# TensorE's order in a group of keys: row scores of the next step ahead of the values product of the preceding group

## Chip, cores, metric

One core of one Trainium2 chip. The metric is device time of one execution, in microseconds; the kernel before ran three times.

## What is computed

A small language model tower on 8 sequences of 1024 tokens, width 512, all in float32:

```python
h = embed(x)                       # gathered frequencies, phases, amplitudes; sin, cos; projection
n = layernorm(h)
Q, K, V = split(n @ q_w.T + q_b), ...          # 16 heads of 32
S = einsum('hid,hjd->hij', K, Q) * SCALE       # K's rows are the rows of the softmax
S = where(i < j, -inf, S) - (i - j)            # causal, with a decay by distance
h = h + softmax(S) @ V @ o_w.T + o_b
h = h + shared_expert(layernorm(h)) + top_6_of_32_experts(layernorm(h))
```

## The kernel before

Three parts run one after the other: `embed`, `attend`, `experts`. The change lies in `attend`.

Attention runs in 32 steps: 8 batches by G = 4 sets g of 4 heads (HG = 4). A step has N_GROUPS = 12 groups m of keys, each a pair (half of the rows, tile j of 128 keys): groups 0 to 3 belong to the first half, groups 4 to 11 to the second. The widths are 512, 384, 256, 128, then 512 five times, then 384, 256, 128. Groups on the diagonal (0 to 3 and 8 to 11) are masked by one more matmul per head.

For each group TensorE (function `step` at L1325) issues:
- `scores` (L1199): keys by rows for each head, K = 32 rows of the array (L1212), the row shift (L1216) and, if masked, the mask (L1222), in four banks of a ring of six.
- `attend_group` (L1225): the values product of the *preceding* group (L1235), out of the exponentials that ScalarE made.
- `row_scores` (L1180): scores of the *next* step, rows by keys (L1188), in four banks of the same ring. VectorE takes their maxima (`row_maxima`, L893, L898), which give the shift of the next step's softmax.
- three gaps A, B, C for dense work in one bank, `ps_dense`, by the tables PROJECT_AT, OUT_AT, QUARTER_AT and so on at L383 to L391: projections of the head set two steps on (L1172 for v, L1176 for q and k), sums of the exponentials (L1244), maxima turned to rows (L1195), and the residual work of the batch before, one quarter of its rows per step: output projection (L1253, g = 0 only), `turn` (L1261), `route` (L1268), `up` (L1276, at m = 6 and 8), `place` (L1292) and `down` (L1284, at m = 11). The first batch has no such residual work.

The bank of the ring decides the waits. Scores of group m take positions 8m to 8m+3, row scores 8m+4 to 8m+7, all modulo 6:

```python
def score_bank(m, h): return ps_ring[(2 * HG * m + h) % RING]
def row_bank(k, h): return ps_ring[(2 * HG * k + HG + h) % RING]
...
if h == 2 and after_exp is not None:
    pe.wait_ge(exp_done, after_exp)
```

So row scores of heads 2 and 3 (L1186) wait for the exponentials of heads 0 and 1 of the same group, and scores of heads 2 and 3 of the next group (L1210) wait for the first two row maxima of this one. Each dense piece waits until the preceding one has been taken out of `ps_dense` (`dense_free`).

ScalarE (`step` at L835) does per group exponentials of heads 0 and 1, gap A, heads 2 and 3 (L776), then at m = 0 and 4 it takes the finished heads (`take_heads`, L783), then gaps B and C. VectorE (`step` at L1104) takes gaps A and B, the four row maxima (L898), a division (L919, L922), then the residual work (`tail_events`: at m = 6 `soft_sum`, L970 to L982; at m = 7 and 10 `gate`, L1056 to L1065; at m = 8 `choose`), then gap C (at m = 7 and 9 the copy of the values, L890; at m = 10 `find_places`, L1030). GpSimd adds the exponentials of a group to those of its first group (L714), four per group, and scatters rows (L718). SyncE moves the residual rows.

Of the kernel before, what the change touches and what calls it, by code (L numbers as in the profile page):

```python
# [36 lines left out]
G = H * HD // P  # L37
HG = H // G
# [15 lines left out]
def wait_from_1(eng, sem, value):  # L54

    if isinstance(value, int) and value <= 0:
        return
    eng.wait_ge(sem, value)
# [309 lines left out]
ITEMS = HG * N_GROUPS  # L368
# [13 lines left out]
A, B, C = range(3)  # L382
# [101 lines left out]
def attend(nc, io, dram):  # L484
    with ExitStack() as ctx:
# [96 lines left out]
        def row_shape(k):  # L582

            i, c = ROW_TILES[k]
            return i, c, c * HALF, min((i + 1) * P, (c + 1) * HALF) - c * HALF
# [4 lines left out]
        def row_bank(k, h):  # L590
            return ps_ring[(2 * HG * k + HG + h) % RING]
# [568 lines left out]
        def _(pe):  # L1160
# [3 lines left out]
            def project(g, kind, half, n):  # L1164

                wait_from_1(pe, dense_free, n)
                w = {"q": q_w, "k": k_w, "v": v_w}[kind]
                if kind == "v":
                    for t in range(NT // 2):
                        tile = half * NT // 2 + t  # L1170
                        for c in range(DC):
                            mm = nc.tensor.matmul(ps_dense[:, t * P:(t + 1) * P], normed_t[:, c, tile * P:(tile + 1) * P],  # L1172
                                                  w[:, c, g * P:(g + 1) * P], start=(c == 0), stop=(c == DC - 1))
                else:
                    for c in range(DC):
                        mm = nc.tensor.matmul(ps_dense[:], w[:, c, g * P:(g + 1) * P], normed_t[:, c, half_cols(half)],  # L1176
                                              start=(c == 0), stop=(c == DC - 1))
                mm.then_inc(dense_full, 1)

            def row_scores(s, g, k, after_exp=None):  # L1180

                i, c, j0, width = row_shape(k)
                wait_from_1(pe, rows_done, ITEMS * s + HG * k)
                for h in range(HG):
                    if h == 2 and after_exp is not None:
                        pe.wait_ge(exp_done, after_exp)  # L1186
                    dims = slice(h * HD, (h + 1) * HD)
                    nc.tensor.matmul(row_bank(k, h)[:, 0:width], k_t[g][dims, i * P:(i + 1) * P],  # L1188
                                     q_t[g][dims, j0:j0 + width], start=True, stop=True).then_inc(rows_full, 1)

            def turn_maxima(s, half, n):
                wait_from_1(pe, dense_free, n)
                pe.wait_ge(max_done, 2 * s + half + 1)
                for i in range(NT // 2):
                    mm = nc.tensor.matmul(ps_dense[:, i * P:(i + 1) * P], max_cols[:, half * NT // 2 + i, :], ident_b[:],  # L1195
                                          start=True, stop=True)
                mm.then_inc(dense_full, 1)

            def scores(st, m):  # L1199

                half, j, i0, width = shape(m)
                masked = j * P == i0
                wait_from_1(pe, exp_done, ITEMS * st.s + HG * m)
                if st.first and m == 0:
                    pe.wait_ge(dense_free, N_PROLOGUE)
                if m == HALF_GROUPS:
                    pe.wait_ge(dense_free, st.number("maxima", 1) + 1)
                for h in range(HG):
                    if h == 2 and (st.rows or m < 2):
                        pe.wait_ge(rows_done, ITEMS * (st.s + 1) + (HG * m - 2 if st.rows or m == 0 else 0))  # L1210
                    dims = slice(h * HD, (h + 1) * HD)
                    nc.tensor.matmul(score_bank(m, h)[:, 0:width], q_t[st.g][dims, j * P:(j + 1) * P],  # L1212
                                     k_t[st.g][dims, i0:i0 + width], start=True, stop=False)
                for h in range(HG):
                    dims = slice(h * HD, h * HD + SHIFT)
                    mm = nc.tensor.matmul(score_bank(m, h)[:, 0:width], key_shift[dims, j * P:(j + 1) * P],  # L1216
                                          row_shift[st.g % 2][dims, i0:i0 + width], start=False, stop=not masked)
                    if not masked:
                        mm.then_inc(scores_full, 1)
                if masked:  # L1220
                    for h in range(HG):
                        nc.tensor.matmul(score_bank(m, h)[:, 0:P], mask_b[:], ident_b[:], start=False,  # L1222
                                         stop=True).then_inc(scores_full, 1)
# [15 lines left out]
            def sum_probs(s, half, n):  # L1239

                wait_from_1(pe, dense_free, n)
                pe.wait_ge(added, ADDS * s + (ADDS if half else EARLY_ADDS))
                for h in range(HG):
                    mm = nc.tensor.matmul(ps_dense[h * HD:(h + 1) * HD, :], ones[:], first_probs[half][h][:],  # L1244
                                          start=True, stop=True)
                mm.then_inc(dense_full, 1)

            def out_project(t, i, n):
                wait_from_1(pe, dense_free, n)

                pe.wait_ge(heads_done, 2 * G * t + 2 * G - (1 if i < NT // 2 else 0))
                for g in range(G):
                    mm = nc.tensor.matmul(ps_dense[:], attn_t[:, g, i * P:(i + 1) * P], o_w[:, g, :],  # L1253
                                          start=(g == 0), stop=(g == G - 1))
                mm.then_inc(dense_full, 1)
# [41 lines left out]
            def of_quarter(x, p, kind, arg, n):  # L1297
                if kind == "turn":
                    turn(x, p, arg, n)
                elif kind == "route":  # L1300
                    route(n)
                elif kind == "up":
                    up(arg, n)
                elif kind == "down":
                    down(x, arg, n)
                elif kind == "place":
                    count_earlier(x, n)

            def dense(st, slot, gap):
                for kind, arg, k in st.uses[slot][gap]:  # L1310
                    n = st.base + k
                    if kind in ("q", "k", "v"):
                        if st.g == 2 and (kind, arg) == PROJECTIONS[0]:
                            pe.wait_ge(normed_in, 16 * (st.b + 2))
                        project((st.g + 2) % G, kind, arg, n)
                    elif kind == "sums":
                        sum_probs(st.s - 1 if arg else st.s, arg, n)
                    elif kind == "maxima":
                        turn_maxima(st.s if arg else st.s + 1, arg, n)
                    elif kind == "out":  # L1320
                        out_project(st.t, arg, n)
                    else:
                        of_quarter(QUARTERS * st.t + st.g, st.g % 2, kind, arg, n)

            def step(st):  # L1325
                for m in range(N_GROUPS):
                    scores(st, m)
                    dense(st, m, A)
                    if m > 0:
                        attend_group(st.s, st.g, m - 1)  # L1330
                    elif not st.first:
                        attend_group(st.s - 1, (st.g - 1) % G, N_GROUPS - 1)
                    dense(st, m, B)
                    if st.rows:
                        row_scores(st.s + 1, (st.g + 1) % G, m, ITEMS * st.s + HG * m + 2)
                    dense(st, m, C)

            pe.wait_ge(normed_in, 16)
            for n, (kind, half) in enumerate(PROJECTIONS * 2):
                project(n // N_PROJ, kind, half, n)  # L1340
                if n >= N_PROJ:
                    for k in range(2):
                        row_scores(0, 0, 2 * (n - N_PROJ) + k)
            turn_maxima(0, 0, N_PROLOGUE - 1)
            for_batches(pe, step)
            attend_group(FINAL - 1, G - 1, N_GROUPS - 1)
            sum_probs(FINAL - 1, 1, EPILOGUE_SUMS)
# [288 lines left out]
```

## Time and profile before

| | us |
|---|---|
| median of 3 runs | 4180.8 (4173.16 to 4185.16) |
| profiled execution | 4192.13 |
| its span | 4190.3 |
| TensorE busy | 3459.1 |
| VectorE busy | 2486.1 |
| GpSimd busy | 1812.4 |
| ScalarE busy | 1043.1 |

A row of the timeline gives the start, the duration, the engine, line, operation, output and inputs, shape and how many instructions it merges; in brackets the idle time of the engine ahead of it and what released it. Matmuls of four heads run side by side, so that a merged row is shorter than the sum of its parts. An fp32 matmul is two instructions (x8 for four heads). The attention part lies between about 615 and 3680 us.

### The profile page before, as it was taken

The page shows a single profiled execution, that of the slowest core. Times are in us where ns is not written, and L with a number is a line of the kernel's source. Part 1 is how long each engine was busy: PE and PEld are TensorE (multiplying, and loading weights), DVE is VectorE, ACT ScalarE, POOL GpSimd, SP SyncE. Part 2 cuts the span into 40 slices and gives each one's busy share as a digit, 9 for nine tenths or more (in the row PEclk, how much of TensorE's full clock was granted, in tenths as well). Part 3 has the DMA queues.
Part 4 walks back from the last instruction along what each step waited for, and adds up shares of the span by engine and source line. Part 5 has one row for each costly group of instructions (what it writes and reads, how often), then busy time and mean ns, then how long its engine had stood idle before and what let it go on. Part 6 is the DMA issues. An engine that isn't in the chain of part 4 may idle for free. (4 is left out here: it accounts for less than half of the span.)

```text
span 4190.3 us, 65616 instructions
## 1 busy us (share of the span) xinstructions
PE 3459.1 (83%) x20360; PEld 1725.1 (41%) x20360; DVE 2486.1 (59%) x6671; ACT 1043.1 (25%) x2427; POOL 1812.4 (43%) x1892
## 2 busy tenths in 40 slices
PE   5676479999888988888898889888988897754998
PEld 1222133444444444343444444444444443233776
DVE  3555434555665676567656665666576567643565
ACT  1111103332332223232223322332232222200111
POOL 3322204544554455355444544554455455522223
PEclk6555589999999999998999999999999997876999
DMA  4444300001111110100011010001000100111997
GB/s 158 142 151 156 146 31 1 26 26 40 63 48 63 41 35 12 49 18 27 22 41 41 11 34 29 31 12 37 26 32 11 46 16 11 44 38 57 264 258 166
DMA packets 123228, 257.99 MB, mean 62 GB/s; under 512 B 38988, under 2 KB 39628, under 8 KB 120192
## 3 DMA queue, kind: packets, MB, share of 16 engines
q1 hardware_dynamic: 78832, 204.56, 14.8%
q0 software_dynamic: 44048, 49.26, 4.7%
q8 instruction: 161, 2.64, 0.3%
q14 instruction: 187, 1.53, 0.1%
HBM read 146.71 MB, written 204.26 MB: 84 GB/s over the span
## 5 line engine op out<-in xcount | busy, mean ns | idle before, releaser
L714 POOL TENSOR_TENSOR a_first_probs<-a_first_probs,a_probs 128x512 f32<-128x512 f32 (+3 forms) x1280 | 1176.0, 953 | 1526.9 <-ACT a_probs L776 943.5
L898 DVE CUSTOM_DVE_ANT_0 a_unused<-a_ps_ring,a_decay 128x512 bf16<-128x512 f32 (+3 forms) x1536 | 773.6, 554 | 593.7 <-PE a_ps_ring L1188 585.0
L776 ACT ACTIVATE a_probs<-a_ps_ring 128x512 f32<-128x512 f32 (+3 forms) x1280 | 505.0, 473 | 752.2 <-PE a_ps_ring L1222 555.5
L718 POOL DMA_INDIRECT d_slots<-a_rows,a_place_i x397 | 394.8, 994 | 250.4 <-DVE a_place_i L1050 142.2
L1212 PE MATMUL a_ps_ring<-a_k_t,a_q_t 32*128 32x512 f32 (+3 forms) x3072 | 416.4, 542 | 71.5 <-DVE a_row_max L898 47.3
L1188 PE MATMUL a_ps_ring<-a_q_t,a_k_t 32*128 32x512 f32 (+3 forms) x3072 | 390.4, 542 | 17.4 <-DVE a_row_max L898 12.4
L1284 PE MATMUL a_ps_dense<-a_sd,a_inner_t 128*128 128x512 f32 x256 | 185.3, 863 | 184.4 <-DVE a_gate_up L1030 181.1
L1176 PE MATMUL a_ps_dense<-a_normed_t,a_q_w 128*128 128x512 f32 x512 | 242.4, 617 | 44.9 <-DMA a_normed_t<-d_normed_t 42.2
L1235 PE MATMUL a_ps_heads<-a_probs,a_values 128*32 128x512 f32 (+3 forms) x2560 | 269.9, 495 | 0.0
L1212 PEld LDWEIGHTS a_ps_ring<-a_k_t,a_q_t 32*128 32x128 f32 x3072 | 146.3, 186 | 275.5 <-issue 147.9
L1253 PE MATMUL a_ps_dense<-a_o_w,a_attn_t 128*128 128x512 f32 x512 | 241.3, 615 | 16.8 <-DVE a_values L890 9.0
L776 ACT ACTIVATE a_first_probs<-a_ps_ring 128x512 f32<-128x512 f32 x256 | 135.7, 605 | 471.0 <-PE a_ps_ring L1222 444.9
L1176 PE MATMUL a_ps_dense<-a_normed_t,a_k_w 128*128 128x512 f32 x512 | 238.5, 609 | 15.9 <-DVE a_residual L929 10.0
L1172 PEld LDWEIGHTS a_ps_dense<-a_v_w,a_normed_t 128*128 128x128 f32 x2048 | 235.1, 193 | 36.5 <-issue 33.8
L1172 PE MATMUL a_ps_dense<-a_v_w,a_normed_t 128*128 128x128 f32 x2048 | 247.3, 279 | 1.6 <-DVE a_values L890 0.9
L919 DVE RECIPROCAL a_sum_inv<-a_sum_inv 128x128 f32<-128x128 f32 x256 | 242.5, 947 | 1.9 <-ACT a_sum_inv L789 1.9
L1188 PEld LDWEIGHTS a_ps_ring<-a_q_t,a_k_t 32*128 32x128 f32 x3072 | 143.4, 187 | 225.1 <-issue 189.2
L1276 PE MATMUL a_ps_dense<-a_rows_t,a_sg 128*128 128x256 f32 x512 | 161.1, 469 | 79.0 <-DVE a_values L890 73.3
L1550 POOL DMA_INDIRECT out<-x_y,x_index x64 | 90.1, 1409 | 236.4 <-DMA out<-x_y,x_index 184.6
L912 DVE CAST a_row_shift<-a_ps_dense 128x512 bf16<-128x512 f32 x64 | 44.2, 691 | 240.6 <-PE a_ps_dense L1195 240.6
L1284 PEld LDWEIGHTS a_ps_dense<-a_sd,a_inner_t 128*128 128x128 f32 x256 | 59.7, 258 | 266.2 <-DVE a_inner_t L1065 150.5
L1276 PEld LDWEIGHTS a_ps_dense<-a_rows_t,a_sg 128*128 128x128 f32 x512 | 112.1, 230 | 125.3 <-DVE a_values L890 76.9
(169 smaller groups left out, 4653.7 us busy)
## 6 DMA issues: line engine op xcount, KB each, us to landing
d_hidden<-e_hidden SPq DMA_DIRECT2D x8, 2048.0 KB, 7.4
d_normed_t<-e_normed_t SPq DMA_DIRECT2D x8, 2048.0 KB, 11.8
a_normed_t<-d_normed_t SPq DMA_DIRECT2D x8, 2048.0 KB, 7.7
a_residual<-d_hidden SPq DMA_DIRECT2D x64, 256.0 KB, 2.7
d_hidden<-a_residual SPq DMA_DIRECT2D x64, 256.0 KB, 2.1
a_hidden<-d_hidden SPq DMA_DIRECT2D x64, 256.0 KB, 2.7
out<-a_hidden SPq DMA_DIRECT2D x64, 256.0 KB, 2.0
x_w_gate<-w_gate SPq DMA_DIRECT2D x32, 512.0 KB, 6.5
```

The source lines that it names most:

```text
L714: nc.gpsimd.tensor_tensor(total_of, total_of, probs_of(m, h)[:, 0:width], ALU.add).then_inc(added, 1)
L718: nc.gpsimd.indirect_dma_start(slot_rows, bass.IndirectOffsetOnAxis(ap=place_i[p][:, j, choice:choice + 1], axis=0), rows[p][:, j, :], Non ...
L776: nc.scalar.activation(probs_of(m, h)[:, 0:width], score_bank(m, h)[:, 0:width], ACT.Exp).then_inc(exp_done, 1)
L898: nc.vector.tensor_tensor_reduce(unused[:, h, 0:width], row_bank(k, h)[:, 0:width], decay[:, at:at + width], 1.0, NEG, ALU.add, ALU.max, r ...
L919: nc.vector.reciprocal(sum_inv[half][:, cols], sum_inv[half][:, cols]).then_inc(sums_inverted, 1)
L1172: mm = nc.tensor.matmul(ps_dense[:, t * P:(t + 1) * P], normed_t[:, c, tile * P:(tile + 1) * P], w[:, c, g * P:(g + 1) * P], start=(c == 0 ...
L1176: mm = nc.tensor.matmul(ps_dense[:], w[:, c, g * P:(g + 1) * P], normed_t[:, c, half_cols(half)], start=(c == 0), stop=(c == DC - 1))
L1188: nc.tensor.matmul(row_bank(k, h)[:, 0:width], k_t[g][dims, i * P:(i + 1) * P], q_t[g][dims, j0:j0 + width], start=True, stop=True).then_i ...
L1212: nc.tensor.matmul(score_bank(m, h)[:, 0:width], q_t[st.g][dims, j * P:(j + 1) * P], k_t[st.g][dims, i0:i0 + width], start=True, stop=False)
L1235: mm = nc.tensor.matmul(ps_heads[dims, at], values[g][:, j, dims], probs_of(m, h)[:, 0:width], start=(j == 0), stop=(j == last_j))
L1276: mm = nc.tensor.matmul(ps_dense[:, k * 2 * P:(k + 1) * 2 * P], w[:, c, m * P:(m + 1) * P], rows_t[:, c, :], start=(c == 0), stop=(c == DC ...
L1284: mm = nc.tensor.matmul(ps_dense[:], inner_t[:, m, j * P:(j + 1) * P], sd[:, m, :], start=(m == 0), stop=(m == MC - 1))
```

## The change

In each group `row_scores` and gap B move ahead of `attend_group`: before, scores, A, values product, B, row scores, C; now, scores, A, row scores, B, values product, C.

```diff
                     scores(st, m)
                     dense(st, m, A)
+                    if st.rows:
+                        row_scores(st.s + 1, (st.g + 1) % G, m, ITEMS * st.s + HG * m + 2)
+                    dense(st, m, B)
                     if m > 0:
                         attend_group(st.s, st.g, m - 1)
                     elif not st.first:
                         attend_group(st.s - 1, (st.g - 1) % G, N_GROUPS - 1)
-                    dense(st, m, B)
-                    if st.rows:
-                        row_scores(st.s + 1, (st.g + 1) % G, m, ITEMS * st.s + HG * m + 2)
                     dense(st, m, C)
```

TensorE, group 8 of a step with g = 1 in the loop over batches, and the `up` piece behind it (L1276), before:

```order
L1216 MATMUL a_ps_ring<-a_row_shift,a_key_shift 128x512 x4
L1222 MATMUL a_ps_ring<-a_ident_b,a_mask_b 128x128 x4
L1235 MATMUL a_ps_heads<-a_probs,a_values 32x512 x4
L58 REGISTER_ALU
L1188 MATMUL a_ps_ring<-a_q_t,a_k_t 128x128 x4
L58 REGISTER_ALU
L1276 MATMUL a_ps_dense<-a_rows_t,a_sg 128x256 x4
```

Now:

```order
L1216 MATMUL a_ps_ring<-a_row_shift,a_key_shift 128x512 x4
L1222 MATMUL a_ps_ring<-a_ident_b,a_mask_b 128x128 x4
L58 REGISTER_ALU
L1188 MATMUL a_ps_ring<-a_q_t,a_k_t 128x128 x4
L1235 MATMUL a_ps_heads<-a_probs,a_values 32x512 x4
L58 REGISTER_ALU
L1276 MATMUL a_ps_dense<-a_rows_t,a_sg 128x256 x4
```

The row scores stand directly behind the mask, and the values product between them and `up`.

TensorE, group 4 of the same step, with the two pieces `turn` (L1261) in gaps A and B and the scores of group 5 behind it, before:

```order
L1261 MATMUL a_ps_dense<-a_ident,a_rows 128x128 x4
L1235 MATMUL a_ps_heads<-a_probs,a_values 32x128 x4
L58 REGISTER_ALU
L1259 REGISTER_ALU
L1261 MATMUL a_ps_dense<-a_ident,a_rows 128x128 x4
L58 REGISTER_ALU
L1188 MATMUL a_ps_ring<-a_q_t,a_k_t 128x512 x4
L1212 MATMUL a_ps_ring<-a_k_t,a_q_t 128x512 x2
```

Now:

```order
L1261 MATMUL a_ps_dense<-a_ident,a_rows 128x128 x4
L58 REGISTER_ALU
L1188 MATMUL a_ps_ring<-a_q_t,a_k_t 128x512 x4
L58 REGISTER_ALU
L1259 REGISTER_ALU
L1261 MATMUL a_ps_dense<-a_ident,a_rows 128x128 x4
L1235 MATMUL a_ps_heads<-a_probs,a_values 32x128 x4
L1212 MATMUL a_ps_ring<-a_k_t,a_q_t 128x512 x2
```

The row scores no longer stand directly ahead of the next group's scores; `turn` and the values product lie between them. The orders of the other four engines are the same.

## Rows read from the trace of the kernel before

**Rows 1.** The page, part 1: busy us, share of the span, instructions.

```profile
PE 3459.1 (83%) x20360; PEld 1725.1 (41%) x20360; DVE 2486.1 (59%) x6671; ACT 1043.1 (25%) x2427; POOL 1812.4 (43%) x1892
```

**Rows 2.** Waits of PE, 700 to 3600 us: total, times, longest.

```profile
PE a_ps_dense L1284 <- DVE a_gate_up L1030: 164.1, 27, 6.3
PE a_ps_dense L1276 <- DVE a_values L890: 73.3, 19, 4.0
PE a_ps_ring L1212 <- DVE a_row_max L898: 42.8, 57, 3.8
```

**Rows 3.** Timeline of PE, group 6 of a step with g = 3.

```profile
2033.67 1.14 PE L1212 MATMUL a_ps_ring<-a_k_t,a_q_t 32*128 32x512 f32 x8
2034.63 0.40 PE L1216 MATMUL a_ps_ring<-a_row_shift,a_key_shift 5*128 5x512 bf16 x4
2034.96 1.07 PE L1235 MATMUL a_ps_heads<-a_probs,a_values 128*32 128x512 f32 x8
2035.95 1.36 PE L1188 MATMUL a_ps_ring<-a_q_t,a_k_t 32*128 32x512 f32 x8
2037.24 1.99 PE L1276 MATMUL a_ps_dense<-a_rows_t,a_sg 128*128 128x256 f32 x8
```

**Rows 4.** Timeline of ACT, exponentials of group 6 of that step.

```profile
2035.05 2.06 ACT L776 ACTIVATE a_probs<-a_ps_ring 128x512 f32<-128x512 f32 x4 [3.83 <-PE a_ps_ring L1216]
```

**Rows 5.** Timelines of PE and of ACT, group 9 of that step.

```profile
2061.78 0.40 PE L1222 MATMUL a_ps_ring<-a_ident_b,a_mask_b 128*128 128x128 bf16 x4
...
2063.10 0.71 PE L1188 MATMUL a_ps_ring<-a_q_t,a_k_t 32*128 32x256 f32 x8
2063.75 3.84 PE L1172 MATMUL a_ps_dense<-a_v_w,a_normed_t 128*128 128x128 f32 x32
...
2062.05 1.64 ACT L776 ACTIVATE a_probs<-a_ps_ring 128x384 f32<-128x384 f32 x4 [0.31 <-PE a_ps_ring L1222]
```

**Rows 6.** Timeline of PE, turn at m = 4 and scores of group 5, same step.

```profile
2022.54 0.66 PE L1261 MATMUL a_ps_dense<-a_ident,a_rows 128*128 128x128 f32 x4 [0.28 <-DVE a_rows L954]
2027.24 0.70 PE L1212 MATMUL a_ps_ring<-a_k_t,a_q_t 32*128 32x512 f32 x2 [0.69 <-DVE a_row_max L898]
```

**Rows 7.** Timeline of PE, `up` at m = 8, same step.

```profile
2055.42 3.68 PE L1276 MATMUL a_ps_dense<-a_rows_t,a_sg 128*128 128x256 f32 x8 [4.00 <-DVE a_values L890]
```

**Rows 8.** Timeline of DVE, from the maxima of group 6 to the values copy.

```profile
2037.26 0.69 DVE L898 CUSTOM_DVE_ANT_0 a_unused<-a_ps_ring,a_decay 128x512 bf16<-128x512 f32 x1 [1.53 <-PE a_ps_ring L1188]
...
2043.05 1.31 DVE L978 TENSOR_TENSOR a_soft<-a_soft_ln,a_soft 128x64 f32<-128x64 f32 x1
...
2053.53 1.24 DVE L1065 TENSOR_SCALAR a_inner_t<-a_gate_e 128x256 f32<-128x256 f32 x1
2054.69 0.68 DVE L890 COPY a_values<-a_ps_dense 128x512 f32<-128x512 f32 x1
```

**Rows 9.** Timeline of DVE, the same lines in the next step, g = 0.

```profile
2155.51 0.22 DVE L978 TENSOR_TENSOR a_soft<-a_soft_ln,a_soft 128x64 f32<-128x64 f32 x1
...
2166.86 0.29 DVE L1065 TENSOR_SCALAR a_inner_t<-a_gate_e 128x256 f32<-128x256 f32 x1
```

**Rows 10.** Timeline of POOL, additions of groups 7 and 8, g = 3.

```profile
2043.03 4.94 POOL L714 TENSOR_TENSOR a_first_probs<-a_first_probs,a_probs 128x512 f32<-128x512 f32 x4
...
2050.55 5.34 POOL L714 TENSOR_TENSOR a_first_probs<-a_first_probs,a_probs 128x512 f32<-128x512 f32 x4 [1.43 <-ACT a_probs L776]
```

**Rows 11.** Timeline of DVE, division at m = 10 (g = 3) and at m = 6 (g = 0).

```profile
2073.39 1.50 DVE L922 TENSOR_TENSOR a_attn_t<-a_attn_t,a_sum_inv 128x128 f32<-128x128 f32 x1
...
2154.09 0.29 DVE L922 TENSOR_TENSOR a_attn_t<-a_attn_t,a_sum_inv 128x128 f32<-128x128 f32 x1
```

**Rows 12.** Timeline of PE, k projection at m = 4, g = 2.

```profile
2326.81 3.70 PE L1176 MATMUL a_ps_dense<-a_normed_t,a_k_w 128*128 128x512 f32 x8 [0.16 <-ACT a_rows_t L800]
```

**Rows 13.** Timeline of PE, output projection at m = 8, g = 0.

```profile
2167.82 3.70 PE L1253 MATMUL a_ps_dense<-a_o_w,a_attn_t 128*128 128x512 f32 x8 [1.30 <-DVE a_values L890]
```

**Rows 14.** Timeline of PE, scores of group 11, first batch.

```profile
684.23 0.38 PE L1212 MATMUL a_ps_ring<-a_k_t,a_q_t 32*128 32x128 f32 x2 [1.06 <-DVE a_row_max L898]
```

## The prediction

> **What bounds the kernel now.** I read the page first: over the whole span TensorE is busy 83%, VectorE 59% [rows 1]. The profiled execution took 4192.1 us (span 4190.3), against a median of 4180.8 for the runs; the sum below is made against 4192.1 and its difference is then taken off the median. Next, the table of waits on PE for 700 to 3600 us [rows 2]: the shared-expert product `down` waits 164.1 us for VectorE, `up` waits 73.3 us in 19 places, key scores wait 42.8 us for row maxima. So inside a group of keys TensorE runs without a gap, and a few times per step it stands for VectorE. I then walked the timeline of one step (the fourth batch, g=3, 1993.68 to 2087.90) and of its neighbours; g=1 and g=3 have the same pattern ("odd steps"). Below, S(m) is the start of the scores of group m.
>
> **What one exchange costs.** Group 6 [rows 3]: scores at 2033.67, shift matmuls at 2034.63, values product at 2034.96, row scores at 2035.95, the next product at 2037.24: 3.57 us. ScalarE starts the four exponentials at 2035.05 and needs 2.06 us, 0.515 each [rows 4]. Row scores of heads 2 and 3 go into the banks of scores 0 and 1, so they wait for two exponentials: 2035.05 + 1.03 + 0.05 = 2036.13. Before, the 0.99 us of the values product covered this. Now row scores of heads 0 and 1 start at 2034.96, heads 2 and 3 at 2036.13; a 512 wide pair takes 1.06 more, then the values product 0.99: 2038.18. Group 6 pays **0.96**, practically the whole values product. Group 9 [rows 5]: mask at 2061.78, exponentials of 384 columns from 2062.05, two of four in 1.64 done at 2062.92, 256 wide row scores to 2063.56, product to 2064.55 where the old order had 2063.75: **0.80**. The same working on the other widths gives 0.36 (m=0), 0.57 (m=2), 0.37 (m=3), 0.98 (m=7), 1.00 (m=8), 0.59 (m=10). Where a dense piece stands in gap A (sums at m=1 and 5, turn at 4, `down` at 11, the output projections of g=0) it covers the exponentials and I cost the exchange at nothing; without that piece it would be 0.4 to 1.0 as above. No instruction is added; DMA, ScalarE, VectorE and GpSimd keep their orders.
>
> **What comes back, odd steps.**
> Groups 0 to 3: nothing; +0.36+0.57+0.37 = +1.3.
> Groups 4 and 5: before, scores(5) started directly behind row scores(4) and its heads 2 and 3 stood until VectorE had two row maxima, at 2027.24 [rows 6]. Now row scores(4) end near 2024.4 (heads 0 and 1 reach VectorE about 2024.2), turn(1) and the 128 wide values product follow, scores(5) starts at 2025.4 and finds its maxima done, ending 2026.7 instead of 2028.5. Sums 0.88, row scores to 2028.95, maxima 0.33, product 0.98, router 1.90 put S(6) at about 2032.1, not 2033.67: -1.57; with 1.3 us already lost, turn(0) no longer waits 0.28 for VectorE. Together -1.85.
> Groups 6 to 8: paid 0.96+0.98+1.00 = 2.94. But `up` of m=8 stands 4.00 us for the copy of the values [rows 7], and behind that stand the granted clock is at its lower level: eight matmuls take 3.68 us where the same eight of m=6 take 1.99 at the upper one [rows 3, 7], and the clock comes back within them: 1.7 lost. Will the copy be early enough? VectorE's chain starts with the row maxima of group 6, at S(6)+3.59 (2037.26), and runs without idle time into the copy, ending near S(6)+21.7 [rows 8]. Row scores of heads 0 and 1 now end at S+2.3, so the chain starts at S(6)+2.45, 1.14 earlier. Its slow operations are slow beside GpSimd's additions: L978 takes 1.31 there and 0.22 in g=0, L1065 1.24 and 0.29 [rows 8, 9]. The additions of group 8 start at S(6)+16.9 now [rows 10] and follow the exponentials, which TensorE's later groups 6 and 7 move to S(6)+18.9; the gate's last three operations then lie ahead of them, 1.15 us in place of 3.4 us. The copy ends about S(6)+18.3, while TensorE only gets there at 17.7+2.94 = 20.6. Stand and low clock go: 2.94-4.00-1.70 = -2.8.
> Groups 9 to 11: VectorE sits idle in group 9 for TensorE, and gets each row maximum 1.0 earlier after S(9) while group 10 starts 0.80 later: the maxima of group 10 start at S(9)+9.7 as before, and `down` in group 11 still stands for this chain, at the lower clock. In it L922 took 1.50 beside GpSimd's last additions and 0.29 elsewhere [rows 11]; these additions start some 0.7 later, so between 0 and -1.2; I take -0.35, since the operation behind L922 can meet them instead.
> Odd step: 1.3-1.85-2.8-0.35 = **-3.7**.
>
> **Other steps.** g=2: group 0 already waits for its exponentials, +0.94 up to group 3. At m=4 the k projection waits for ScalarE's turned rows, before 0.16 [rows 12]; ScalarE takes the heads ahead of them, and the heads' last values product now comes after turn(1), so this wait grows: +0.8 together with m=5. Then -2.8-0.35: **-1.4**. g=0: the same +0.8, then the stand of 1.30 at the output projection of m=8 [rows 13] shrinks by 1.0 and the row maxima of m=10 come 0.8 earlier: **-1.0**. A batch: 2 x -3.7 - 1.4 - 1.0 = -9.8, six full batches -59. Last batch: its `up` stands little, some groups gain, some pay: 0. First batch, without residual work: exposures 0.57+0.37+0.36+1.10+0.35+0.80+0.36 = 3.9, against waits of PE for row maxima that go (1.06 [rows 14], 0.69 twice, 0.44): +1 per step, +4. **Sum: -59 + 4 = -55 us**: 4137 for the profiled execution, 4126 for the median.
>
> **A rule weighed.** L978 lasts 1.31 us while additions run on GpSimd and 0.22 without [rows 8, 9]. The Trainium skill ("SBUF — State Buffer", section on the two separate sides) says that VectorE and GpSimd lock a shared port pair for a whole instruction, the other one blocking fully; the two rows agree. It speaks against this change where more of the chain falls into additions: a rival below.
>
> **The rivals.**
> (1) Forecast, 4126: chance 0.54.
> (2) More operations blocked: the chain starts earlier against the additions of group 6, so that L970, L972, L975 and L1056 each take 1.0 more. Copy at S(6)+22.3, `up` stands 1.7 without losing the clock: 18 x 1.7 = +31, 4157. For: L978 to L982 do it today. Against: L1065 and L1061 leave the additions. 0.10. By the page on SBUF of the Trainium skill each meeting costs up to a whole addition, here 4.94/4 = 1.24 us [rows 10]; the stand would be 2.6 and the time 4173.
> (3) The clock stays down: short stands in every group lower TensorE's activity and the granted clock of groups 6 to 9 falls as it does now: 18 x 1.7 = +31, 4157. Against: its clock is full through the present groups with stands of 0.7. 0.14.
> (4) Slower: the exposures are paid and the values copy is no earlier. Its place is the 18 stands of `up` at m=8: if GpSimd's additions hold VectorE's chain so that the copy ends at S(6)+21.7 again, S(9) stays where it is and only the small terms are left: odd -0.55, g=2 +1.7, g=0 +0.8, batch +1.4; six batches and the first: +13, 4194. It decides once the copy gains less than 0.7 us. 0.10.
> (5) Larger gain: L922's block is gone everywhere (-0.85 more in 24 steps): -20, 4105. 0.12.
> That the change does nothing is excluded by the order on PE.
>
> **Numbers.** The range goes from (5) with some more, 4090, to past (2) and (3), 4172; (4) is left out above. A measurement here tells 0.3% (12.5 us) from no change. Slower by more takes most of (4): 0.09; within 0.07; faster 0.84.
>
> **What would show it.** Right: the wait of L1276 for L890 (19 times) nearly gone and the granted clock of that stretch at full; the wait of L1212 for L898 below 15 us; a new wait of L1188 for ScalarE's L776, some 0.2 us each, and row scores taking over 2 us from first to last; L898 starting 2.45 us behind the scores; `down` standing as before, about 5.5 us. Wrong: L1276 still waiting over 2 us (4), or a stretch at half clock without a long stand ahead of it (3).

## The result, and the profile after

The changed kernel takes 4268.9 us (median of 4 runs, 4264.3 to 4274.9) against 4178.7 for the kernel before (with a fourth run): ratio 1.0216, 95% interval 1.0194 to 1.0238. It is **2.2% slower**, where 4126 us was forecast. Its profiled execution has a span of 4263.4 us. Part 1 of its page, against [rows 1]:

```profile
PE 3571.5 (84%) x20360; PEld 1763.6 (41%) x20360; DVE 2566.6 (60%) x6671; ACT 1048.8 (25%) x2427; POOL 1822.0 (43%) x1892
```

The instruction counts are unchanged, but VectorE is busy 80.5 us longer. An operation that is held back counts as busy, so this is the first hint. The table of waits of PE, 700 to 3600 us, against [rows 2] (total, times, longest):

```profile
PE a_ps_dense L1284 <- DVE a_gate_up L1030: 157.6, 26, 6.3
PE a_ps_dense L1276 <- DVE a_values L890: 54.7, 19, 3.0
PE a_ps_ring L1188 <- ACT a_probs L776: 30.9, 87, 0.7
PE a_ps_dense L1176 <- ACT a_rows_t L800: 15.7, 13, 1.3
PE a_ps_ring L1188 <- ACT a_first_probs L776: 13.8, 25, 0.6
PE a_ps_ring L1212 <- DVE a_row_max L898: 6.3, 19, 1.7
```

Row maxima are waited for 6.3 us instead of 42.8, as forecast. Row scores now wait for ScalarE, which was forecast too, at some 0.2 us each; it is 0.4. What fails is the second row: `up` still waits for the values copy in the same 19 places, 2.9 us each, and after the exposed exponentials have been paid.

**Where the time went, by group.** The starts of the scores (L1212) give the length of each group. Means over the six full batches of the profiled executions, us, change minus before (the twelfth column runs to the next step's scores):

```
step   m=0   1     2     3     4     5     6     7     8     9     10    11     sum   forecast
g=0   -0.73 +0.14  0.00 -0.84 +0.83 +0.35  0.00  0.00 -1.00  0.00 +0.64 -1.13  -1.7   -1.0
g=1   +0.36 +0.14 +0.64 +0.42 -0.11 -1.35 +0.99 +0.99 +1.38 +0.85 +0.64 -1.41  +3.5   -3.7
g=2    0.00 -0.12 +0.64 +0.43 +0.82 +0.35 +0.99 +1.00 +1.85 +0.85 +0.29 -0.97  +6.1   -1.4
g=3   +0.36 +0.14 +0.64 +0.42 -0.10 -1.35 +1.00 +1.00 +1.33 +0.85 +0.64 -1.62  +3.3   -3.7
```

A batch is 11.2 us longer, six are 67 us; the first batch adds 1.4, and the first scores start 3.4 later (614.7, 618.1). That is 72 of the 73.1 us between the two spans. The 3.4 us need not be due to the change: in experiments 1 to 10, none of which touches the part ahead of attention, the first scores start anywhere between 607.1 and 619.3. Column m=8 carries the surprise: in g=1 to 3 it should have been about -4.7, and is +1.3 to +1.9.

The timeline of PE in the same step as [rows 3, 7] (fourth batch, g=3; S(6) = 2064.89):

```profile
2064.89 1.14 PE L1212 MATMUL a_ps_ring<-a_k_t,a_q_t 32*128 32x512 f32 x8
...
2067.40 1.13 PE L1188 MATMUL a_ps_ring<-a_q_t,a_k_t 32*128 32x512 f32 x4 [0.31 <-ACT a_probs L776]
2068.45 1.07 PE L1235 MATMUL a_ps_heads<-a_probs,a_values 128*32 128x512 f32 x8
...
2082.82 0.70 PE L1212 MATMUL a_ps_ring<-a_k_t,a_q_t 32*128 32x512 f32 x2 [0.26 <-DVE a_row_max L898]
...
2090.01 3.61 PE L1276 MATMUL a_ps_dense<-a_rows_t,a_sg 128*128 128x256 f32 x8 [3.02 <-DVE a_values L890]
```

Group 6 pays just the 1.0 us that was worked out. But `up` of m=8 stands 3.02 us, and its eight matmuls take 3.61 us, much as in [rows 7]. The stand is 0.98 us shorter than before, and still group 8 takes 13.83 us instead of 12.53. Two terms make up for it: its own exposed exponentials, 1.0 us, and 1.4 us in its scores, whose heads 2 and 3 now meet late row maxima of group 7 (the mask matmuls start 2.66 us behind S(8), where it was 1.29). VectorE and GpSimd show why; first VectorE, against [rows 8]:

```profile
2070.92 3.62 DVE L922 TENSOR_TENSOR a_attn_t<-a_attn_t,a_sum_inv 128x128 f32<-128x128 f32 x1
...
2075.39 5.19 DVE L975 TENSOR_TENSOR a_soft<-a_soft,a_soft_w 128x64 f32<-128x64 f32 x1
2080.62 0.29 DVE L978 TENSOR_TENSOR a_soft<-a_soft_ln,a_soft 128x64 f32<-128x64 f32 x1
...
2088.12 1.23 DVE L1065 TENSOR_SCALAR a_inner_t<-a_gate_e 128x256 f32<-128x256 f32 x1
2089.28 0.68 DVE L890 COPY a_values<-a_ps_dense 128x512 f32<-128x512 f32 x1
```

Then GpSimd's additions of groups 5, 6 and 7:

```profile
2063.33 4.93 POOL L714 TENSOR_TENSOR a_first_probs<-a_first_probs,a_probs 128x512 f32<-128x512 f32 x4 [10.96 <-PE a_ps_heads L1235]
...
2069.42 4.95 POOL L714 TENSOR_TENSOR a_first_probs<-a_first_probs,a_probs 128x512 f32<-128x512 f32 x4
2074.54 0.99 POOL L718 DMA_INDIRECT d_slots<-a_rows,a_place_i  x1 [0.17 <-issue]
2075.54 4.95 POOL L714 TENSOR_TENSOR a_first_probs<-a_first_probs,a_probs 128x512 f32<-128x512 f32 x4
```

In the kernel before, the same two engines (S(6) = 2033.67):

```profile
2030.71 4.94 POOL L714 TENSOR_TENSOR a_first_probs<-a_first_probs,a_probs 128x512 f32<-128x512 f32 x4 [10.59 <-PE a_ps_heads L1235]
...
2036.81 4.97 POOL L714 TENSOR_TENSOR a_first_probs<-a_first_probs,a_probs 128x512 f32<-128x512 f32 x4
...
2040.70 1.24 DVE L922 TENSOR_TENSOR a_attn_t<-a_attn_t,a_sum_inv 128x128 f32<-128x128 f32 x1
...
2042.80 0.22 DVE L975 TENSOR_TENSOR a_soft<-a_soft,a_soft_w 128x64 f32<-128x64 f32 x1
```

Read the ends. L922 ends some 0.16 us behind the end of group 6's four additions in both kernels (2074.54 and 2074.37; 2041.94 and 2041.78). L975 of the change ends at 2080.58, behind the last addition of group 7 (2080.49): an operation of 0.22 us waited out a whole run of four. The copy so ends at S(6)+25.1, where 18.3 was forecast and 21.7 was before.

And read the starts. The run of group 5 begins 2.96 us ahead of the scores of group 6 before, and 1.56 us after. It is released by the values product of group 4, by these lines of `add_probs` (group 5 has j = 1; other lines are left out):

```python
if j == 1:
    pool.wait_ge(attended, N_GROUPS * st.s + m)
...
for h in range(HG):
    pool.wait_ge(exp_done, ITEMS * st.s + HG * m + h + 1)
```

In group 5 that is the product which the change moved behind the row scores. The runs of groups 6 and 7 follow with only one scatter (L718, 0.99 us) between them. It is the rule and not this step: in each of the 18 steps with g=1 to 3 of the six full batches the run of group 5 starts 2.96 us ahead of S(6) before and 1.56 now, and L975 lasts 0.22 to 0.23 us before and 5.19 to 5.21 now. Over all its 32 executions L975 went from 12.6 to 102.0 us.

### The profile page after: what moved, and what is told of

Same layout as the page of the kernel before. It is cut to its first block and busy times, and to the rows that moved or that the text cites. A ratio compares the mean times of both kernels' runs of the same rounds, so it can differ in the third digit from the quotient of the medians.

```text
span 4263.4 us, 65610 instructions
## 1 busy us (share of the span) xinstructions
PE 3571.5 (84%) x20360; PEld 1763.6 (41%) x20360; DVE 2566.6 (60%) x6671; ACT 1048.8 (25%) x2427; POOL 1822.0 (43%) x1892
## 5 line engine op out<-in xcount | busy, mean ns | idle before, releaser
L1188 PE MATMUL a_ps_ring<-a_q_t,a_k_t 32*128 32x512 f32 (+3 forms) x3072 | 528.9, 542 | 60.3 <-ACT a_probs L776 32.7
L718 POOL DMA_INDIRECT d_slots<-a_rows,a_place_i x397 | 396.7, 999 | 250.9 <-DVE a_place_i L1050 142.9
L1212 PE MATMUL a_ps_ring<-a_k_t,a_q_t 32*128 32x512 f32 (+3 forms) x3072 | 395.3, 542 | 27.6 <-DVE a_row_max L898 10.0
L1188 PEld LDWEIGHTS a_ps_ring<-a_q_t,a_k_t 32*128 32x128 f32 x3072 | 201.3, 189 | 332.3 <-issue 152.4
L1176 PE MATMUL a_ps_dense<-a_normed_t,a_k_w 128*128 128x512 f32 x512 | 240.2, 612 | 21.6 <-ACT a_rows_t L800 15.7
L1212 PEld LDWEIGHTS a_ps_ring<-a_k_t,a_q_t 32*128 32x128 f32 x3072 | 133.0, 185 | 224.5 <-issue 158.5
L1276 PE MATMUL a_ps_dense<-a_rows_t,a_sg 128*128 128x256 f32 x512 | 167.6, 484 | 60.3 <-DVE a_values L890 54.7
L922 DVE TENSOR_TENSOR a_attn_t<-a_attn_t,a_sum_inv 128x128 f32<-128x128 f32 x256 | 165.1, 645 | 13.6
L1276 PEld LDWEIGHTS a_ps_dense<-a_rows_t,a_sg 128*128 128x128 f32 x512 | 117.2, 241 | 132.7 <-DVE a_values L890 74.2
```

What stands on the lines that cost most here:

```text
L718: nc.gpsimd.indirect_dma_start(slot_rows, bass.IndirectOffsetOnAxis(ap=place_i[p][:, j, choice:choice + 1], axis=0), rows[p][:, j, :], Non ...
L1276: mm = nc.tensor.matmul(ps_dense[:, k * 2 * P:(k + 1) * 2 * P], w[:, c, m * P:(m + 1) * P], rows_t[:, c, :], start=(c == 0), stop=(c == DC ...
```

## The experiments

Two theories stood. Port (P in the first texts, R, as "release", in the last ones): VectorE's waits beside GpSimd's additions take back what groups 6 to 8 should give. Exposure (E): the exposed exponentials cost more than was summed.

**1, 2: additions of 128 columns.** Both orders, with the additions of groups 6 and 7 cut from 512 to 128 columns, so that these two kernels leave out most of those additions and their softmax sums are not the right ones:

```
                 at = slice(HALF - width, HALF)
+                if m in (6, 7):
+                    width, at = 128, slice(HALF - 128, HALF)
```

> The order of the change, and GpSimd's additions of groups 6 and 7 act on 128 of the 512 columns (the rest of these sums is left out). Theory P (port): the values copy is late in the changed kernel because L922 (3.6 us) and L975 (5.2 us) wait out whole runs of additions. With short runs the copy ends near S(6)+19, the stand of `up` at m=8 (3.02 us) and its clock loss go, and the stretch S(6) to S(9) falls from 30.4 to 24.3 us in 18 steps: about 4160 us. Theory E (the exposed exponentials alone cost the time): the stretch keeps its stand, 4255 to 4270 us.

> The order of before with the same short additions of groups 6 and 7 (part of these sums left out). Theory P: four VectorE operations lose 1.0 us each, the copy ends near S(6)+17.6, the stand of 4.0 us shrinks to about nothing and the clock stays up: S(6) to S(9) from 27.1 to about 21.4 us, some 4080 us. The distance between this run and e1 is then the bare price of the exposed exponentials, 50 to 80 us. Theory E: 4170 to 4180.

New order 4136.7 us (ratio 0.9883, 0.9852 to 0.9913), old order 4067.9 (0.9727, 0.9662 to 0.9792). The wait of `up` for the values copy is gone from both. Theory P had asked for some 4160 and 4080. Short additions are worth 132 us to the new order and 111 to the old. With them out of the way the new order costs 69 us net: the exposed exponentials where there is no stand at m=8 to take away, less what the new order gains elsewhere (1.35 us in group 5 of each odd step, for one).

**3: the new order in all groups but 6 to 8.** In this and the next ones the order has both forms, and a condition chooses:

```
+                    rows_first = m < 6 or m > 8
                     scores(st, m)
                     dense(st, m, A)
+                    if st.rows and rows_first:
+                        row_scores(st.s + 1, (st.g + 1) % G, m, ITEMS * st.s + HG * m + 2)
+                    if rows_first:
+                        dense(st, m, B)
...
+                    if not rows_first:
+                        dense(st, m, B)
+                    if st.rows and not rows_first:
```

> The new order in groups 0 to 5 and 9 to 11, the old one in groups 6 to 8. Theory P: the loss sits in groups 6 to 8, and what is left is the rest of the change: per batch about -2 (g=0), -1 for each odd step, +2 (g=2): 4165 to 4185 us. Theory E: each exposed group costs its 0.4 to 0.8 us wherever it is, +2.7 us in 18 steps: about 4225 us.

4286.6 us (1.0250, 1.0184 to 1.0316): slower than the full change, and both theories missed. Groups 6 and 7 are as before, and group 8 is 3.1 to 4.6 us longer than before. Its L975 takes 111.9 us in all. So the block is not made by the order in groups 6 to 8, but brought to them from ahead: here too the run of group 5 starts 1.56 us ahead of S(6).

**4, 5: a gap between additions.** Each addition waits for the end of the one before it, in both orders:

```
-                    wait_from_1(pool, added, ADDS * st.s + HG * (later(m) - 1) + h + 1)
+                    wait_from_1(pool, added, ADDS * st.s + HG * later(m) + h)
```

> The order of the change, and every addition on GpSimd waits for the one before it, so that they are not queued back to back. Theory P with a lock that GpSimd keeps only while its next addition is already waiting: L922 and L975 get in after one addition (at most 1.3 us), the copy ends near S(6)+20, the stand goes: about 4165 us. If VectorE is held for the whole run all the same, or under theory E: 4265 to 4285 us.

> The order of before, and every addition on GpSimd waits for the one before it (the edit of e4). Theory P: in the order of before no VectorE operation waits for more than one addition, so the gaps give little there: 4160 to 4185 us, and the new order with gaps (4133) is then really the faster one. Rival: the gaps help either order by the same 130 us: about 4050 us.

The new order falls to 4133.0 us (0.9883, 0.9821 to 0.9944); the old one rises to 4234.8 (1.0126, 1.0106 to 1.0146). Both forecasts missed: 4165 and 4160 to 4185 were expected. In the six full batches no operation of the chain lasts over 2 us any more, and the longest of all is 2.1; L975 is 0.84 us in the median of the new order. But several are now held by an addition that they meet. In the new order the copy is in time all the same, at S(6)+18.6, and group 8 takes 7.76 us, 4.7 to 5.0 less than before. In the old one L972, L975, L978, L980 and L982 last 1.2 to 2.0 us each, the copy ends at S(6)+23.8 or later, and group 8 grows by 2.1 to 3.0 us.

**6: a mixture by the small terms.** `rows_first = m < 8 if st.t is None else st.g == 0 or (st.g % 2 == 1 and m == 4)`: the new order in group 4 of the steps g=1 and 3, in all groups of g=0, and in groups 0 to 7 of the first batch.

> The new order only in all groups of g=0 with residual work, in group 4 of g=1 and g=3, and in groups 0 to 7 of the first batch; elsewhere the order of before. Theory P: values product 4 in group 5 and with it GpSimd's additions keep their place before the scores of group 6, nothing is blocked for a whole run; g=0 gains 2.7, odd steps 1.5 each: -5.7 per batch and a few us in the first: 4140 to 4150 us. If group 4 in the new order is enough to shift the additions into VectorE's chain: 4200 or more.

4183.2 us over 10 runs (1.0005, 0.9993 to 1.0018): nothing, where 4140 to 4150 was expected. Group 5 of the odd steps gives its 1.33 us, but group 8 of the steps g=1 to 3 takes 0.6 to 0.8 back, g=0 gains 1.4 us instead of 2.7, and g=2 loses 1.9. Without the gain at m=8 the rest is worth little.

**7, 8: all groups but 5, and only 6 to 8.** `rows_first = m != 5` and `rows_first = m >= 6 and m <= 8`.

> The new order in all groups but 5, where the values product of group 4 (which releases GpSimd's additions of group 5) keeps its place ahead of the row scores. Theory P with this release as the cause: the additions of groups 5 to 7 run 1.4 us earlier against the scores of group 6, L922 or L975 lose at most one addition each: 4150 to 4220 us. If the release is not what matters: 4265 us as the change.

> The new order only in groups 6 to 8 of every step. Theory P with the release of GpSimd in group 5 as the cause: additions stay in place, VectorE's chain starts 1.1 us earlier and meets only the end of the additions of group 6; the stand of `up` at m=8 shrinks by what the exposures (2.9 us) add: 4120 to 4190 us. If starting VectorE's chain earlier is by itself what gets it blocked: 4240 us or more.

4138.2 us (0.9897, 0.9871 to 0.9922; 4150 to 4220 expected) and 4134.6 (0.9888, 0.9858 to 0.9918), two runs each, as in experiments 2 to 4. **Taking one group of twelve out of the change turns +2.2% into -1.0%.** In both, groups 6, 7 and 8 of the odd steps stand at +1.00, +0.99, -4.73: -2.74 us, where -2.8 was forecast. The chain of experiment 8, g=3 of the fourth batch, S(6) = 2001.93, VectorE, GpSimd, TensorE:

```profile
2011.06 0.23 DVE L975 TENSOR_TENSOR a_soft<-a_soft,a_soft_w 128x64 f32<-128x64 f32 x1
...
2011.84 0.20 DVE L982 TENSOR_SCALAR a_soft<-a_soft 128x64 f32<-128x64 f32 x1
...
2019.21 0.68 DVE L890 COPY a_values<-a_ps_dense 128x512 f32<-128x512 f32 x1
...
1998.98 4.93 POOL L714 TENSOR_TENSOR a_first_probs<-a_first_probs,a_probs 128x512 f32<-128x512 f32 x4 [10.58 <-PE a_ps_heads L1235]
...
2012.29 5.00 POOL L714 TENSOR_TENSOR a_first_probs<-a_first_probs,a_probs 128x512 f32<-128x512 f32 x4 [1.09 <-ACT a_probs L776]
...
2022.60 1.99 PE L1276 MATMUL a_ps_dense<-a_rows_t,a_sg 128*128 128x256 f32 x8
```

Group 5's run starts 2.95 us ahead of S(6). GpSimd then has to wait 1.09 us for the exponentials of group 7, and in that hole L975 to L982 pass at 0.2 us each. The copy ends at S(6)+17.96, TensorE finds it done, and the eight matmuls take 1.99 us.

**9: only group 5 in the new order** (`rows_first = m == 5`).

> The order before, with the new order in the one group m=5 of every step: there the values product of group 4, which releases GpSimd's additions of group 5, comes after the row scores. Theory R (the moved release alone does it): those additions start some 1.4 us nearer to the scores of group 6 (1.55 us ahead of them, where it was 2.96), L975 or L922 waits out a whole run of four additions in the steps g=1 to 3, group 8 grows from 12.5 us by 3 to 5.5 us in each, as in the kernel with the new order in all groups but 6 to 8: 54 to 99 us in six batches, 4235 to 4280 us. Rival A (it takes the new order in the groups 0 to 4 or 9 to 11 as well): nothing but the exposed exponentials of one group, 4175 to 4195 us.

4278.2 us (1.0217, 1.0191 to 1.0243): one group is enough for a loss as large as that of the whole change. The same view of it, S(6) = 2077.53, with TensorE:

```profile
2075.98 4.95 POOL L714 TENSOR_TENSOR a_first_probs<-a_first_probs,a_probs 128x512 f32<-128x512 f32 x4 [12.17 <-PE a_ps_heads L1235]
...
2084.56 2.65 DVE L922 TENSOR_TENSOR a_attn_t<-a_attn_t,a_sum_inv 128x128 f32<-128x128 f32 x1
2088.07 5.19 DVE L975 TENSOR_TENSOR a_soft<-a_soft,a_soft_w 128x64 f32<-128x64 f32 x1
...
2095.50 0.70 PE L1212 MATMUL a_ps_ring<-a_k_t,a_q_t 32*128 32x512 f32 x2 [2.27 <-DVE a_row_max L898]
```

The additions start 1.55 us ahead of S(6). Group 5 itself costs only 0.17 to 0.36 us, since the sums in gap A cover its exponentials; group 8 grows by 3.7 to 4.5.

The block is the same, but it is paid for in another place than in the whole change, so that the equal totals are in part chance. TensorE reaches the scores of group 8 earlier against VectorE's chain and stands 2.27 us for the row maxima of group 7, where it stood 0.26 in the change. The granted clock falls behind that stand and is at its lower level (0.50 of full) from 2096.2 to 2106.4, 10.2 us; in the kernel before it was so for 3.4 us of the same step (2055.5 to 2058.9), behind the stand of `up`. The waits of PE (700 to 3600 us) for row maxima and for the values copy come to 115.9 us here and 116.1 before, so the loss is not in their sum; it goes with the longer stretch at the lower clock. In experiments 3 and 11 the clock is low for 10.2 and 13.7 us of this step.

**11, 12: GpSimd alone made late.** TensorE's order untouched (the old one, and that of experiment 8); GpSimd runs 2, 4 and 6 tiny chained additions on a scratch tile ahead of those of group 5 in the steps g=1, 2 and 3:

```
+                if m == 5:
+                    for k in range(2 * st.g):
+                        nc.gpsimd.tensor_tensor(idle, idle, idle, ALU.add).then_inc(idled, 1)
+                        pool.wait_ge(idled, 12 * st.b + st.g * (st.g - 1) + k + 1)
```

> The order before, TensorE untouched; GpSimd alone runs 2, 4 and 6 tiny chained additions on a scratch tile ahead of the additions of group 5 in the steps g=1, 2 and 3, each an estimated 0.25 to 0.3 us, so that these start about 0.5, 1.1 and 1.6 us later. Theory R: at the delay that is nearest to 1.4 us, VectorE's L922 and L975 wait out whole runs of additions (3 to 5 us) though no TensorE instruction has moved, and group 8 grows by 2 us or more; at the smallest delay it need not. Rival A (the block comes of TensorE's order): L922 stays under 1.6 us and L975 at 0.22 us, group 8 within 1.5 us of 12.5 in all three.

> The new order in the groups 6 to 8 alone, the version of 4134.6 us, with the same delays of GpSimd in the steps g=1, 2 and 3. Theory R: at a delay near 1.4 us L975 takes some 5 us again, the copy of the values comes late and group 8 grows from 7.76 us to 13 or more, what the full change shows. Rival A: group 8 stays within 1.5 us of 7.76 in all three steps.

One execution each: 4245.6 and 4214.1 us, so that the evidence here is the traces and not these times. The additions of group 5 start 0.56, 1.13 and 1.70 us later in g=1, 2 and 3. In the fourth batch, group 8 and L975 (L981 in these two):

```
                  old order: group 8   L975      new 6 to 8: group 8   L975
no delay          12.53                0.22      7.76                  0.23
g=1, 0.56 late    15.32                5.20      7.76                  0.22
g=2, 1.13 late    15.66                5.19      12.57                 0.23
g=3, 1.70 late    18.34                5.19      14.20                 5.18
```

Over the six full batches L975 is as in the table in every step, to 0.02 us. Group 8 varies in the old order: 15.3 to 15.7, 15.7 to 16.1, 15.9 to 18.3; in the other one it is 7.76, 11.1 to 12.6, 14.2 to 15.5.

From experiment 12, VectorE and GpSimd, g=2 and then g=3:

```profile
1963.40 0.23 DVE L981 TENSOR_TENSOR a_soft<-a_soft,a_soft_w 128x64 f32<-128x64 f32 x1
1963.66 1.28 DVE L984 TENSOR_TENSOR a_soft<-a_soft_ln,a_soft 128x64 f32<-128x64 f32 x1
...
2059.05 5.18 DVE L981 TENSOR_TENSOR a_soft<-a_soft,a_soft_w 128x64 f32<-128x64 f32 x1
...
2059.20 4.94 POOL L720 TENSOR_TENSOR a_first_probs<-a_first_probs,a_probs 128x512 f32<-128x512 f32 x4
```

So the cause is shown without moving a single instruction of TensorE: additions that start late make the block. The old order has no room, since 0.56 us is enough; the order with the hole in groups 6 to 8 stands 0.56 and fails at 1.13, there with the division (L928 here, L922 above) held for 3.35 us and single additions behind it (1.28 us on L984, 1.2 on the two that follow), at 1.70 with a whole run. I had thought that 0.56 us might be harmless in the old order too.

**10: the parts that pay.** `rows_first = st.t is not None and ((m >= 6 and m <= 8) or (st.g % 2 == 1 and m == 4))`: groups 6 to 8 behind the first batch, where experiment 8 had lost 11 us, and group 4 of the odd steps.

> The new order only in the groups 6 to 8 of the steps behind the first batch, and in group 4 of the steps g=1 and 3. The kernel with 6 to 8 alone took 4134.6; its first batch was 11 us longer than before's, which goes; group 4's new order takes 1.4 us out of group 5 in two steps of each of six batches, 17 us. Theory R (nothing here moves GpSimd's additions of group 5 against the scores of group 6): 4105 to 4115 us. Rival A (the shift by group 4 meets the gate's chain elsewhere, as group 8 of g=1 grew by 1.1 us where group 4 alone was changed): 4120 to 4135 us.

**4109.9 us**, 5 runs (4104.9 to 4110.9), ratio 0.9820, 0.9801 to 0.9839: 72 us below the kernel before, and below all versions that compute the whole. A batch is 13.1 us shorter, 2.7 of it in group 5 of the two odd steps, where the stand of [rows 6] has gone.

## Why the prediction was wrong

**The step that failed** is the one on groups 6 to 8: "The copy ends about S(6)+18.3". What TensorE pays and gets back was sized right (paid 0.96 and 0.98 in groups 6 and 7, measured 1.00 and 0.99; net -2.8, measured -2.74 in experiments 7 and 8), but it comes only while GpSimd's runs lie where they lay. The text said "DMA, ScalarE, VectorE and GpSimd keep their orders", which is so, and took the order for the times: the values product was costed as work that is moved on TensorE, and not as a release. In group 5 it releases a run of GpSimd that then goes on back to back through three groups. That cost +1.38 and +1.33 in place of about -4.7 at m=8, 6.1 us a step, and 6.6 in g=2: over 18 steps some 113 of the 143 us between 4126 and 4269. Of the rest, 13 us are the other groups of these batches (a whole batch: +11.2, where -9.8 was forecast). 15 more are no fault of the sum: it was made against a profiled execution 11 us above its median, while that of the change lies 4 below its own.

That the copy ends at S(6)+17.96 in experiment 8, where 18.3 was worked out, is in part luck. Two terms came out: the chain starts 1.20 us earlier (forecast 1.14), and the gate's last three operations save 2.2 (forecast 2.25). The others were not in the sum and nearly cancel: L978, L980 and L982 are held for no addition and save 3.0, while L922 takes 1.0 longer, L1056 0.7, and the row maxima wait 0.9 for row scores of the late group 7 and heads 2 and 3.

The kernel before could have warned. In its last batch, which the rows did not cover, VectorE is held for a run, or the rest of one, already: L1061 for 4.42 us (3531.93), L972 for 5.57 (3599.03) and L975 as follows:

```profile
3605.09 5.63 DVE L975 TENSOR_TENSOR a_soft<-a_soft,a_soft_w 128x64 f32<-128x64 f32 x1
3605.68 4.96 POOL L714 TENSOR_TENSOR a_first_probs<-a_first_probs,a_probs 128x512 f32<-128x512 f32 x4
```

**Rival (2)** named the right mechanism, with a wrong size: one addition for each of four operations, at most 1.24 us. Measured were 3.6 us for one and 5.2 us for another. **Rival (4)** gave the right sign and its condition, a copy that gains less than 0.7 us, was met: it ended 3.4 us later than before. It was priced at +13 with a chance of 0.10 because I let the copy be at worst as late as before; that it could gain less than nothing was not considered. The range ended at 4172 because (4) was left out of it, and its 4194 would have been 75 us short too.

**Rival (3)**, the clock: refuted. The granted clock of 900 to 3600 us is 0.95 in the change and 0.93 before, and groups 6 and 7 run at full clock.

**What held.** The chain starts 2.39 us behind S(6), forecast 2.45. Groups 0 to 3 of the odd steps: +1.56, forecast +1.3. Groups 4 and 5: -1.46, forecast -1.85. Row scores wait for ScalarE, 44.7 us in 112 places. Row maxima: 6.3 us, forecast under 15. Groups 4 and 5 of g=2: +1.17, forecast +0.8. Groups 9 to 11 of the odd steps: 0.0 instead of -0.35. The first batch: +1.4 for +4. g=0: -1.7 for -1.0, by luck: m=8 gave the -1.00 that was worked out, but groups 0 and 3 gave 1.6 us that were in no sum, groups 4 and 5 cost 1.2 instead of 0.8, and groups 9 to 11 gave 0.5 instead of 0.8.

## What to carry to other kernels

When an instruction is moved, list the semaphores that it increments and who waits on them, on engines too that are far from the critical path; the work that it releases moves with it. Where two engines hold each other off, price a shift of one against the other from both sides, and try the change group by group: here one of twelve groups made +2.2% out of a kernel that was ready to give -1.0%. And look in all steps of the old trace for the rare times that an operation takes long: three holds in the last batch showed at what price VectorE can meet GpSimd.

## What the runs showed of the hardware

A VectorE operation that meets a run of GpSimd additions can be held for the whole rest of the run: 5.19 us for an operation of 0.22, behind four additions of 1.24. The Trainium skill ("SBUF — State Buffer", the section on the two sides) has the pair of ports locked for the length of an instruction; these rows go beyond one instruction, and the measurement decides. Elsewhere the same operations pass after one addition each (1.31, 1.19, 1.16 us for L978, L980, L982 before).

What decides between the two is open. In the 18 steps each L975 of the change that was held for 5.2 us was recorded 0.14 to 0.16 us ahead of the run's first addition, and 0.23 to 0.24 us ahead it passed in the kernel before. The distance alone does not decide: in the six steps g=2 of experiment 12 it passed at 0.14 to 0.16, and the L975 of 5.63 us above was recorded 0.59 us ahead. In one step of the change L975 passed and the next operation was held instead:

```profile
3509.64 0.23 DVE L975 TENSOR_TENSOR a_soft<-a_soft,a_soft_w 128x64 f32<-128x64 f32 x1
3509.97 4.86 DVE L978 TENSOR_TENSOR a_soft<-a_soft_ln,a_soft 128x64 f32<-128x64 f32 x1
...
3509.78 4.96 POOL L714 TENSOR_TENSOR a_first_probs<-a_first_probs,a_probs 128x512 f32<-128x512 f32 x4
```

With recorded gaps of some 0.08 us between additions (four take 5.3 to 5.4 us instead of 4.94, experiments 4 and 5) no such long hold is left. Why a gap has this effect no run shows.
